# The second 32-column attention: softmax sums and values in bf16 high and low parts instead of fp32

## The chip, the cores and the metric

The kernel runs on one core of a Trainium2 chip. The metric is the device time of one execution in microseconds (us). A core has five engines that run their own instruction streams and meet only at semaphores: TensorE (PE; its weight loads are PEld), VectorE (DVE), ScalarE (ACT), GpSimd (POOL) and SyncE (SP, which starts most DMAs).

## The reference, cut to what matters

The whole kernel is four layers of cross attention and feed forward on x (16 batches of 128 tokens, 128 wide) with a context of 77 keys per batch. The change touches one part, the second attention of the third layer:

```python
# H, D = 16, 32; y is the context: 77 keys of 64 numbers in each of 16 batches
q = jnp.einsum('bsc,hcd->bhsd', xn, wq)
k = jnp.einsum('btc,hcd->bhtd', yn, wk)
v = jnp.einsum('btc,hcd->bhtd', yn, wv)
a = jax.nn.softmax(jnp.einsum('bhsd,bhtd->bhst', q, k) * D ** (-0.5), axis=-1)
o = jnp.einsum('bhst,bhtd->bhsd', a, v)
o = o.transpose(0, 2, 1, 3).reshape(x.shape[0], x.shape[1], H * D)
x_out = x + o @ li1_w + li1_b
```

## The kernel before, in words

The program is a list of stages: L0x, L0m, L1x, L1f, L2a1, L2f1, **L2a2** (this attention), L2f2, L2m, L3x, L3m. All stages write their instructions for each engine by hand; the order in which a function such as `attention` calls its parts is the order on that engine. L2a1 and L2a2 have heads of 32 columns (`A.upright`), L1x has heads of 64.

In a stage of attention a loop runs b from 0 to 19, and each part works on a batch that lags behind it. For L2a2 iteration b holds on TensorE, in this order: `values(b-1)` (v of a batch), `key_scores(b-2)` (L876 and L893, scores in four PSUM banks `ST`), `row_maxima(b, (0, 1))` (L850), `sums(b-3)` (L924: the exponentials times a matrix of ones and zeros, `fourths`, 16 products with fp32 operands), `turn_maxima(b-1)` (L861), up to two projections of a later group of batches, `turned(b-3)` (L940: v times the exponentials, 16 fp32 products), `out_project(b-4)` (L740, 12 products and one of the bias), `row_maxima(b, (2, 3))` (L850), `spread(b-3)` (L952: the reciprocals of the sums, spread over the heads), and one late projection. Projections exist in b = 1 to 3, 5 to 7 and 9 to 11. A product with an fp32 operand leaves two records in the profile, so 16 of them show as x32.

ScalarE makes the exponentials of a batch in two halves (L1598, 77x1024 each), keeps them in fp32 in one of four buffers (`A.PF`), and evacuates PSUM. VectorE does in iteration b: `row_maxima(b, (0, 1))` (L2180 twice), `sums(b-3)` (L2189, the reciprocal, then L2190, the low part of it, with both inputs in SBUF), the low parts of the early projections (L2039), `out_project(b-4)` (L2226, the residual), L2180 twice again for banks 2 and 3, `turned(b-3)` (L2199, outputs times reciprocals). GpSimd does `outputs_lo` (L2857, the low part of the scaled outputs, for which `out_project` on TensorE waits), and now and then `rstd` (L2786 and L2788) for the layer norms. In L1x GpSimd also splits the exponentials: `exponentials_lo` (L2839) takes fp32 exponentials and their upper halves and writes the low halves in bf16.

Apart from the score banks, all results on TensorE go through four PSUM banks in turn. `take` gives a product the next bank and waits until what was in it four takes ago has been read:

```python
def take(*key):
    t = turns.n
    turns.one()
    K.turn[key] = t
    sem.wait_ge(K.emptied[t % 4], t // 4)
    return K.work[t % 4]
```

The takes of an iteration without projections are v, max 0, max 1, sum, negm, o, out, max 2, max 3, scale. So max 2 comes four takes behind sum, whose bank L2190 sets free. With one early projection out is four takes behind sum, with two it is o.

Four records of TensorE that work on different column groups of 32 start together (L924, L940, L952: the four values of i); this text calls them a round.

## Time and profile before

| | |
|---|---|
| median of 3 runs | 1186.53 us (1183.08 to 1191.68) |
| profiled execution | 1188.89 us |
| its span in the profile | 1187.1 us |
| busy in the span: PE / DVE / ACT / POOL | 885.7 / 825.1 / 710.4 / 555.2 us |
| granted TensorE clock, mean of the span | 0.864 |
| batches of L2a2 in full flow | 691 to 796 us of the span |

A row of the timeline is start, length, engine, line, operation, output and inputs by name (`area` is one large SBUF tensor out of which most buffers are cut), shapes, number of instructions merged, and in brackets the idle time before it and what ended it. A merged row's length is from the first start to the last end, and neighbouring rows of a pipelined engine overlap; so what a group costs TensorE is the distance from its start to the start of the next group. A row of --source type gives the minimum, median and maximum length in ns.

### The profile page before, as it was taken

Reading aid. Unit: us, or ns where it says so; the run is one execution under the profiler, and the core shown is the slowest. Engines: PE = TensorE matmul, PEld = TensorE weight load, DVE = VectorE, ACT = ScalarE, POOL = GpSimd, SP = SyncE. Lnnn points to the kernel's source line nnn. Section 1 sums busy time; section 2 is a strip of 40 time slices with the busy share of each in tenths; the row PEclk is TensorE's granted clock in tenths of the full one; section 3 lists DMA queues with packets and bytes.
Section 4 is the critical chain, followed back from the end, with each engine's and each line's share of the span. In section 5 each row is a group of like instructions: output and inputs, shape, how many; then the busy total and the mean of one; then the engine's idle time right before and its main releaser. Section 6 shows DMA issues by size and latency. Waiting matters only on the chain.

```text
span 1187.1 us, 35741 instructions
## 1 busy us (share of the span) xinstructions
PE 885.7 (75%) x14275; PEld 670.4 (56%) x14340; DVE 825.1 (70%) x2234; ACT 710.4 (60%) x1441; POOL 555.2 (47%) x580
## 2 busy tenths in 40 slices
PE   3687658879998664788888488988389865787683
PEld 2465547736777444366666266765278733565573
DVE  4676747888877796678867577757556848666563
ACT  5877546765655665675566566557367684764331
POOL 3474755465567345254452322222551575657334
PEclk9788869988999877799999699989689967876697
DMA  4331142230110101000001000000142221110133
GB/s 110 95 92 31 51 108 80 64 80 28 30 38 20 43 12 49 24 21 12 4 4 46 1 3 4 4 3 2 33 128 73 66 76 41 37 37 24 52 99 88
DMA packets 63040, 53.75 MB, mean 45 GB/s; under 512 B 13915, under 2 KB 51291, under 8 KB 62685
## 3 DMA queue, kind: packets, MB, share of 16 engines
q1 hardware_dynamic: 57100, 42.25, 12.6%
q0 software_dynamic: 4096, 8.40, 2.4%
q8 instruction: 119, 1.95, 0.7%
q10 hardware_dynamic: 1683, 0.81, 0.3%
q14 instruction: 42, 0.34, 0.1%
HBM read 34.22 MB, written 16.25 MB: 43 GB/s over the span
## 4 chain that ended last, share of the span: by engine, by line
PE 36%; DVE 28%; ACT 13%; issue 11%; POOL 7%; DMA 4%; POOLq 1%; ACTq 0%; SPq 0%; DVEq 0%
PE psum L740 12%; PE psum L1324 4%; POOL sorted_in L2990 3%; DVE area L2039 3%; PE psum L1342 2%; DVE stats L2020 2%; PE psum L882 2%; DVE negm L2180 2%; DVE x L2582 1%; DVE area L2212 1%; ACT area L1414 1%; PE psum L964 1%; PE psum L747 1%; ACT xn L1438 1%; DMA area<-sorted_in 1%
## 5 line engine op out<-in xcount | busy, mean ns | idle before, releaser
L1414 ACT ACTIVATE area<-psum 128x512 bf16<-128x512 f32 (+2 forms) x164 | 85.6, 537 | 127.1 <-PE psum L740 66.6
L2039 DVE TENSOR_TENSOR area<-psum,area 128x512 bf16<-128x512 f32 (+3 forms) x156 | 92.7, 618 | 40.0 <-ACT area L1414 38.5
L2793 POOL TENSOR_TENSOR moe<-stage,moe 128x512 bf16<-128x512 f32 x47 | 54.3, 1157 | 110.9 <-ACT moe L1409 110.9
L1598 ACT ACTIVATE area<-psum 77x1024 f32<-77x1024 f32 (+1 forms) x96 | 92.7, 1016 | 22.1 <-PE psum L893 14.4
L2693 DVE TENSOR_TENSOR area<-area 128x512 bf16<-128x512 f32 x106 | 73.9, 702 | 43.8 <-ACT area L1937 31.3
L1324 PE MATMUL psum<-xT_hi,moe 128*128 128x128 bf16 x848 | 98.2, 226 | 5.9 <-issue 3.0
L2786 POOL TENSOR_SCALAR rstd<-moments 128x4 f32<-128x4 f32 (+1 forms) x49 | 13.4, 274 | 153.5 <-DVE moments L2024 150.4
L1324 PE MATMUL psum<-xT_lo,moe 128*128 128x128 bf16 x424 | 84.2, 226 | 0.0
L1342 PE MATMUL psum<-moe,area 128*128 x424 | 83.8, 278 | 0.2
L1324 PEld LDWEIGHTS psum<-xT_hi,moe 128*128 x848 | 76.2, 102 | 10.9 <-issue 7.8
L2920 POOL TENSOR_TENSOR area<-area 128x640 bf16<-128x640 f32 x64 | 79.2, 1259 | 0.5 <-ACT area L1764 0.5
L2180 DVE TENSOR_REDUCE negm<-psum 128x4 bf16<-128x512 f32 (+1 forms) x128 | 68.3, 576 | 13.9 <-PE psum L850 13.5
L1344 PE MATMUL psum<-moe,area 128*128 x424 | 77.4, 222 | 0.0
L2857 POOL TENSOR_TENSOR area<-area 128x512 bf16<-128x512 f32 x32 | 33.3, 1039 | 92.5 <-DVE area L2199 82.6
L2818 POOL DMA_INDIRECT area<-sorted_out,row_index x32 | 35.3, 1103 | 66.7 <-DMA sorted_out<-area 57.9
L1937 ACT ACTIVATE area<-psum,L2be 128x128 f32<-128x128 f32 x184 | 52.5, 368 | 22.4 <-PE psum L1324 22.3
L2839 POOL TENSOR_TENSOR area<-area 77x1024 bf16<-77x1024 f32 x32 | 60.2, 1899 | 6.5 <-ACT area L1598 6.5
L2039 DVE TENSOR_TENSOR xT_lo<-psum,xT_hi 128x512 bf16<-128x512 f32 (+1 forms) x44 | 29.4, 667 | 46.5 <-ACT xT_hi L1414 46.5
L2788 POOL TENSOR_TENSOR rstd<-rstd,cols 128x4 f32<-128x4 f32 (+1 forms) x53 | 59.5, 1123 | 4.4
L2363 DVE TENSOR_REDUCE area<-psum 128x4 bf16<-128x320 f32 x128 | 55.6, 479 | 6.6 <-PE psum L1094 6.6
L740 PE MATMUL psum<-area 128*128 128x128 bf16 (+1 forms) x512 | 45.9, 249 | 18.4 <-DVE area L2474 13.7
L740 PEld LDWEIGHTS psum<-area 128*128 128x128 bf16 (+1 forms) x512 | 42.4, 135 | 23.2 <-issue 22.1
(276 smaller groups left out, 3050.1 us busy)
## 6 DMA issues: line engine op xcount, KB each, us to landing
area<-sorted_in SPq DMA_DIRECT2D x22, 256.0 KB, 3.8
sorted_out<-area SPq DMA_DIRECT2D x22, 256.0 KB, 2.3
stage<-in_w_L0m SPq DMA_DIRECT2D x16, 256.0 KB, 2.8
stage<-in_w_L2m SPq DMA_DIRECT2D x16, 256.0 KB, 2.8
stage<-in_w_L3m SPq DMA_DIRECT2D x16, 256.0 KB, 2.7
sorted_in<-area SPq DMA_DIRECT2D x2, 1472.0 KB, 7.3
stage<-in_w_L2a SPq DMA_DIRECT2D x8, 320.0 KB, 3.4
stage<-in_w_L1x SPq DMA_DIRECT2D x6, 320.0 KB, 3.0
```

What stands on the lines that cost most here:

```text
L740: ins = pe.matmul(out, lhsT, rhs, start=i == 0, stop=i == len(terms) - 1)
L1324: ins = pe.matmul(bank[:, S * c:S * c + S], lhsT, v, start=n == 0, stop=n == 2)
L1342: pe.matmul(both, h_hi, R.w2[c][:, bass.ds(at_w[tile] * 2, 2 * D)], start=R.b2 is None and c == 0, stop=c == FC - 1, skip_group_check=True)
L1344: ins = pe.matmul(high, h_lo, R.w2[c][:, bass.ds(at_w[tile] * 2, D)], start=False, stop=c == FC - 1, skip_group_check=True)
L1414: ins = act.activation(out, bank, ACT.Copy)
L1598: act.activation(A.PF[n % 4][0:A.L, :].rearrange("p (k n) -> p k n", k=2), K.ST[0:A.L, 2 * half:2 * half + 2, :], ACT.Exp, scale=A.scale). ...
L2039: ins = dve.tensor_tensor(out, bank, high, ALU.subtract)
L2180: empty(dve.tensor_reduce(out, bank_of(key)[:, 0:4 * L].rearrange("p (h l) -> p h l", h=4), AX.X, ALU.max, negate=True), key)
L2693: dve.tensor_tensor(R.HL[u], R.HF[u], upper(R.HF[u]), ALU.subtract).then_inc(K.tile_split, tiles.one())
L2788: pool.tensor_tensor(r, r, K.col("half", 0, n)[parts, :], ALU.pow).then_inc(K.rstd_ready, 1)
L2839: pool.tensor_tensor(A.PL[n % 4][0:A.L], A.PF[n % 4][0:A.L, :].rearrange("p (h q) -> p h q", h=8), A.PH[n % 4][0:A.L], ALU.subtract).then_ ...
L2920: pool.tensor_tensor(A.PL[n % 4], A.PF[n % 4], A.PH[n % 4], ALU.subtract).then_inc(K.p_split, 1)
```

## The change

Only L2a2 is changed (`splits=2`; L3x counts its own splits one place later). `A.apart` turns the following on: GpSimd runs `exponentials_lo` for both halves of each batch, as in L1x, between the instructions that it had. VectorE gets `values_lo(b-2)`, which subtracts from the fp32 values their upper halves (77x512, both inputs in SBUF) and sits behind the first pair of row maxima. TensorE's `sums` multiplies `fourths` with the high and the low parts in bf16 (32 products), and its `turned` makes three products for each head: high by high, high by low, low by high (48 products); both wait for `p_split`, and `turned` for `values_apart`.

```diff
+        self.apart = self.upright and splits is not None
+        if self.apart:
+            n = H * hd
+            self.V_hi = [upper(K.carve(V_AT + n * s, n)).rearrange("p (h d) -> p h d", h=H) for s in range(3)]
+            self.V_lo = [K.carve(at, n // 2, BF16).rearrange("p (h d) -> p h d", h=H)
+                         for at in (V_AT + 3 * n, V_AT + 3 * n + n // 2, TMP_AT)]
+            self.fourths_hi = upper(K.carve(OT_AT + n + 384, 128)).rearrange("p (r n) -> p r n", r=4)
...
# TensorE, sums(b)
                 sem.wait_ge(K.exp_done, A.half0 + n + 1)
+                if A.apart:
+                    sem.wait_ge(K.p_split, A.split0 + n + 1)
+                    for k, part in enumerate((A.PH, A.PL)):
+                        for i in range(4):
+                            ins = pe.matmul(bank[32 * i:32 * i + 32, 0:S], A.fourths_hi[0:L, r, :],
+                                            part[n % 4][0:L, 4 * (r % 2) + i, :], start=r == k == 0, stop=r == 3 and k == 1,
+                                            skip_group_check=True)
+                    continue
...
# TensorE, turned(b)
+            if A.apart:
+                sem.wait_ge(K.values_apart, b + 1)
...
+                if A.apart:
+                    sem.wait_ge(K.p_split, A.split0 + n + 1)
+                    v_hi, v_lo, p_hi, p_lo = A.V_hi[b % 3], A.V_lo[b % 3], A.PH[n % 4], A.PL[n % 4]
+                    for k, (v, p) in enumerate(((v_hi, p_hi), (v_hi, p_lo), (v_lo, p_hi))):
+                        for i in range(4):
+                            ins = pe.matmul(bank[32 * i:32 * i + 32, S * c:S * c + S], v[0:L, 4 * c + i, :],
+                                            p[0:L, 4 * (c % 2) + i, :], start=k == 0, stop=k == 2, skip_group_check=True)
+                    continue
...
# VectorE
+        def values_lo(b):
+            for a, _ in A.value_parts():
+                sem.wait_ge(*K.emptied_at((name, "v", b, a)))
+            if b >= 3:
+                sem.wait_ge(K.filled, K.fill[name, "o", b - 3, 0])
+            s = b % 3
+            dve.tensor_tensor(A.V_lo[s][0:A.L], A.Vs[s][0:A.L], A.V_hi[s][0:A.L], ALU.subtract).then_inc(K.values_apart, 1)
...
                 row_maxima(b, (0, 1))
...
+            if A.apart and 0 <= b - 2 < B:
+                values_lo(b - 2)
...
# GpSimd
-        split = mask if A.keys_from_x else exponentials_lo if not A.upright else None
+        split = mask if A.keys_from_x else exponentials_lo if A.apart or not A.upright else None
...
-                       prepare=Normed(K.base, K.res2, wd("ln2g"), wd("ln2b"), 1, also=K.x), affine0=12)
+                       prepare=Normed(K.base, K.res2, wd("ln2g"), wd("ln2b"), 1, also=K.x), affine0=12, splits=2)
-    K.L3x = Dense(K, "L3x", 4, 1, K.x, late=K.L2m, splits=2)
+    K.L3x = Dense(K, "L3x", 4, 1, K.x, late=K.L2m, splits=3)
```

GpSimd's order in the middle of L2a2, before (L2857 is `outputs_lo`, L2802 and L2810 the next group's normed tokens, L2786 and L2788 `rstd`):

```order
L2857 TENSOR_TENSOR area<-area 128x512 x3
L2802 TENSOR_TENSOR area<-area,wide 128x512
L2810 TENSOR_TENSOR x<-x,area 128x512
L2857 TENSOR_TENSOR area<-area 128x512
L2786 TENSOR_SCALAR rstd<-moments 128x4
L2788 TENSOR_TENSOR rstd<-rstd,cols 128x4
L2857 TENSOR_TENSOR area<-area 128x512 x6
```

The same place in the changed kernel, where lines are numbered anew (L2876 is `exponentials_lo`, L2894 `outputs_lo`, L2823 and L2825 `rstd`):

```order
L2894 TENSOR_TENSOR area<-area 128x512
L2876 TENSOR_TENSOR area<-area 77x1024 x2
L2839 TENSOR_TENSOR area<-area,wide 128x512
L2847 TENSOR_TENSOR x<-x,area 128x512
L2894 TENSOR_TENSOR area<-area 128x512
L2876 TENSOR_TENSOR area<-area 77x1024
L2823 TENSOR_SCALAR rstd<-moments 128x4
L2825 TENSOR_TENSOR rstd<-rstd,cols 128x4
L2876 TENSOR_TENSOR area<-area 77x1024
L2894 TENSOR_TENSOR area<-area 128x512
L2876 TENSOR_TENSOR area<-area 77x1024 x2
```

Two splits now stand behind each `outputs_lo`, and where the statistics of the next group come, `rstd` stands between the two splits of a batch.

VectorE's order in one iteration without projections, before:

```order
L2180 TENSOR_REDUCE negm<-psum 128x4 x2
L2189 RECIPROCAL area<-psum 128x128
L2190 TENSOR_TENSOR area<-area 128x128
L2226 TENSOR_TENSOR area<-area,psum 128x128
L2180 TENSOR_REDUCE negm<-psum 128x4 x2
L2199 TENSOR_TENSOR area<-area,psum 128x512
```

And in the changed kernel (L2215 is the row maxima, L2195 `values_lo`, L2224 and L2225 the reciprocal and its low part):

```order
L2215 TENSOR_REDUCE negm<-psum 128x4 x2
L2195 TENSOR_TENSOR area<-area 77x512
L2224 RECIPROCAL area<-psum 128x128
L2225 TENSOR_TENSOR area<-area 128x128
L2261 TENSOR_TENSOR area<-area,psum 128x128
L2215 TENSOR_REDUCE negm<-psum 128x4 x2
L2234 TENSOR_TENSOR area<-area,psum 128x512
```

`values_lo` now stands ahead of the reciprocal; all else is in its old order.

## Rows read from the trace of the kernel before

**Rows 1.** Windows: length, busy us (instructions) by engine, granted clock, DMA share, GB/s.

```profile
691.00:796.00 105.00, 94.35 (x2976) 73.30 (x2978) 75.31 (x182) 67.26 (x118) 25.45 (x29) 0.97 0.02 4
```

**Rows 2.** Timeline of PE, iteration b = 12.

```profile
754.27 0.30 PE L850 MATMUL psum<-area 32*128 32x77 bf16 x8
754.50 1.08 PE L924 MATMUL psum<-area 77*32 77x128 f32 x32
755.40 0.24 PE L861 MATMUL psum<-ident_bf,negm 128*32 128x128 bf16 x4
755.46 1.06 PE L940 MATMUL psum<-area 77*32 77x128 f32 x32
756.45 0.84 PE L740 MATMUL psum<-w_b,area 128*128 128x128 bf16 x12
...
757.29 0.31 PE L850 MATMUL psum<-area 32*128 32x77 bf16 x8
757.53 0.64 PE L952 MATMUL psum<-area,ident_bf 128*32 128x128 bf16 x32
758.09 0.63 PE L740 MATMUL psum<-w_b,ctx2T 128*77 128x512 bf16 x2
...
759.57 0.30 PE L850 MATMUL psum<-area 32*128 32x77 bf16 x8
```

**Rows 3.** Timeline of DVE, the same iteration.

```profile
754.61 0.86 DVE L2180 TENSOR_REDUCE negm<-psum 128x4 bf16<-128x308 f32 x2 [0.65 <-PE psum L850]
755.65 0.96 DVE L2189 RECIPROCAL area<-psum 128x128 f32<-128x128 f32 x1 [0.18 <-PE psum L861]
756.64 0.29 DVE L2190 TENSOR_TENSOR area<-area 128x128 bf16<-128x128 f32 x1
758.41 0.68 DVE L2199 TENSOR_TENSOR area<-area,psum 128x512 f32<-128x512 f32 x1
```

**Rows 4.** Timeline of ACT and POOL, the same iteration.

```profile
754.48 1.93 ACT L1598 ACTIVATE area<-psum 77x1024 f32<-77x1024 f32 x2 [0.43 <-PE psum L893]
...
759.17 1.04 POOL L2857 TENSOR_TENSOR area<-area 128x512 bf16<-128x512 f32 x1 [4.51 <-DVE area L2199]
```

**Rows 5.** Instructions of one line: the split of exponentials in L1x.

```profile
L2839 POOL TENSOR_TENSOR area<-area x32: 1882/1890/1990, 258.1 to 382.3; 77x1024 bf16<-77x1024 f32 x32
```

**Rows 6.** Timeline of DVE: a low part of 512 columns from two SBUF inputs.

```profile
733.60 0.69 DVE L2143 TENSOR_TENSOR xT_lo<-xT,xT_hi 128x512 bf16<-128x512 f32 x1 [1.35 <-ACT xT_hi L1551]
```

**Rows 7.** Instructions of L2190: in L2a1 (480 to 625 us), then in L2a2 (663 to 796 us).

```profile
L2190 DVE TENSOR_TENSOR area<-area x16: 291/814/970, 509.9 to 618.8; 128x128 bf16<-128x128 f32 x16
...
L2190 DVE TENSOR_TENSOR area<-area x16: 291/292/1107, 694.0 to 791.8; 128x128 bf16<-128x128 f32 x16
```

**Rows 8.** Timelines of POOL and DVE where they meet, in L2a1 and then L1x.

```profile
550.62 2.13 POOL L2848 TENSOR_SCALAR_AFFINE_SELECT area<-area 128x1024 f32<-128x1024 f32 x2 [1.07 <-ACT area L1598]
551.94 0.95 DVE L2190 TENSOR_TENSOR area<-area 128x128 bf16<-128x128 f32 x1
...
256.62 1.16 POOL L2793 TENSOR_TENSOR moe<-stage,moe 128x512 bf16<-128x512 f32 x1 [7.67 <-ACT moe L1409]
256.66 1.66 DVE L2576 TENSOR_TENSOR x<-x,moe 128x512 f32<-128x512 f32 x1
258.08 3.84 POOL L2839 TENSOR_TENSOR area<-area 77x1024 bf16<-77x1024 f32 x2 [0.31 <-ACT area L1598]
```

**Rows 9.** Timeline of DVE and PE in b = 10, PE and POOL in b = 7.

```profile
743.45 0.29 DVE L2190 TENSOR_TENSOR area<-area 128x128 bf16<-128x128 f32 x1
...
743.80 1.08 PE L940 MATMUL psum<-area 77*32 77x128 f32 x32 [0.33 <-DVE area L2190]
...
723.14 0.85 PE L740 MATMUL psum<-w_b,area 128*128 128x128 bf16 x12 [0.86 <-DVE area L2190]
...
722.32 1.04 POOL L2788 TENSOR_TENSOR rstd<-rstd,cols 128x4 f32<-128x4 f32 x1
```

**Rows 10.** Timeline of PE in b = 14.

```profile
769.98 1.44 PE L740 MATMUL psum<-w_b,area 128*128 128x128 bf16 x12 [1.25 <-POOL area L2857]
```

More of the change, by code:

```diff
@@ L263, in __init__ @@
         self.var_ready, self.rstd_ready, self.p_split = sem("var_ready"), sem("rstd_ready"), sem("p_split")
+        self.values_apart = sem("values_apart")
         self.p_masked, self.w_split, self.shifted = sem("p_masked"), sem("w_split"), sem("shifted")
@@ L466, in __init__ @@
         self.half0 = 2 * B * number
-        if not self.upright:
+        self.apart = self.upright and splits is not None
+        if splits is not None:
             self.split0 = 2 * B * splits
+        if self.apart:
[3 more added lines that the diff above has]
+                         for at in (V_AT + 3 * n, V_AT + 3 * n + n // 2, TMP_AT)]
+            assert 4 * n <= 2 * V_N
+            self.fourths_hi = upper(K.carve(OT_AT + n + 384, 128)).rearrange("p (r n) -> p r n", r=4)
     def affine_of(self, g, keys):
```

## The prediction

> **What bounds the kernel now.** I looked first at the windows view of the stretch of L2a2 in which batches flow: TensorE is busy for 94.35 of 105 us, VectorE for 75.31, GpSimd for 25.45, at a granted clock of 0.97 [rows 1]. That says that TensorE is full and GpSimd has room, but not which wait decides, so I read the timeline of one iteration without projections, b = 12. TensorE goes through it without a gap: its first maxima start at 754.27 and those of the next iteration at 759.57, a period of 5.30 us [rows 2]. VectorE has waits of its own there, and its L2190 ends at 756.93, 0.36 before TensorE comes to the second maxima at 757.29, for which that end sets the bank free [rows 2, 3]. So TensorE bounds this iteration, and VectorE is 0.36 us from bounding it. In iterations with projections that reserve is gone already: in b = 10 the value products start 0.06 after the end of L2190 and had waited 0.33 for it, and in b = 7 the output product waited 0.86 for it [rows 9].
>
> **What the change takes away.** In fp32 the sums cost 754.50 to 755.40, 0.90 us for 8 rounds, so 0.112 a round; the value products cost 755.46 to 756.45, 0.99 for 8 rounds, so about 0.10 more where column groups give way to full width [rows 2]. L952 is the nearest bf16 form: 8 rounds and the same step to full width in 0.56, so 0.057 a round [rows 2]. The sums become 8 bf16 rounds, 0.46, and save 0.44. The values become 12 rounds, 0.68 and 0.10, and save 0.21. That is 0.65 a batch, 10.4 us over 16 batches: all that there is to win, 0.9% of the time.
>
> **What it adds.** GpSimd gets 32 splits of 77x1024 at 1.89 us [rows 5], 60 us in all; with `outputs_lo` at 1.04 [rows 4] a batch costs it 4.82. That is under the period, so by its own load it is no bound. VectorE gets 16 times `values_lo`. Its form is not in this stage, but L2143, 512 columns from two SBUF inputs, takes 0.69, of which about 0.61 is not overlapped [rows 6]. It stands between the maxima and the reciprocal.
>
> **Where the two meet.** L2190 takes 0.29 us when alone. In L2a1, where GpSimd masks exponentials at the time, its median is 0.81 [rows 7]. One instance shows why: the masks ran 550.62 to 552.75, L2190 was started at 551.94 and ended at 552.89, 0.14 after them [rows 8]. L2576 in L1x, also with two SBUF inputs, was started 0.04 after a GpSimd instruction and ended at 258.32, 0.54 after that one's end at 257.78 [rows 8]. So a VectorE instruction with two SBUF inputs stands still until a reading GpSimd instruction ends. In the other direction, the two L2839 behind it took 3.84 where two of 1.89, overlapping by 0.04, make 3.74: GpSimd, started at 258.08, lost 0.10, so it was let in about 0.14 before VectorE's end [rows 5, 8]. The page "SBUF — State Buffer" of the Trainium skill (section "Who interferes with whom") says that the first to issue holds the shared port pair for the whole instruction; the row has it given back a little earlier. By the page each split would start 0.14 later than I put it, and the sum would be some 2 us higher.
>
> **b = 12 again, changed,** with 754.27 as zero [rows 2, 3, 4]. The maxima end at 1.20 and let the next instruction in at 1.12. `values_lo` runs 1.12 to 1.81. The first half of the exponentials, begun at 0.21, ends at about 1.22 (half of 1.93, with the overlap); GpSimd could start 0.08 later, at 1.30, but gets in at 1.67 and runs to 3.56. The reciprocal runs 1.73 to 2.69. L2190 is started at 2.71, meets the split and ends at 3.56 + 0.14 = 3.70. The second maxima on TensorE start at 3.8, instead of 757.29, which is 3.02. From there to the next first maxima it was 2.28, and still is: 6.08 against 5.30, **0.8 us longer**, though TensorE's own work got 0.65 shorter. Nothing runs over: VectorE's L2199 comes to its end at about 5.6, the second split at 5.6, `outputs_lo` at 6.7, before `values_lo` of the next iteration (7.2) and before the next output product needs it.
>
> **The same for the other iterations.** b = 12, 13 and 15 have this shape: 3 x 0.8 = 2.4. In b = 10 `values_lo` puts the reciprocal 0.34 later, L2190 is started at 743.78 instead of 743.45, the split that began about 742.74 holds it to 744.77, and the value products start at 744.85 instead of 743.80 [rows 9]; they are 0.21 shorter, so the iteration is 0.8 longer. I take that for b = 5, 6, 9, 10, 11: 4.0. In b = 3 and 7 GpSimd's order has `rstd` between the two splits, where L2190 will arrive; its longer part is 1.04 [rows 9], so I take 1.8 each: 3.6. In b = 4 and 14 `rstd` precedes `outputs_lo` on GpSimd and TensorE waits for that already (1.25 us in b = 14 [rows 10]); L2190 meets a split instead of `outputs_lo`: between 0 and 1.89, I take 1.0 each: 2.0. In b = 8 ScalarE holds `spread` back and hides it: 0. In the last three sum iterations there are no maxima, TensorE gains and the two splits of the last batch come in between the exponentials and the sums: +0.4. The sum is **12.4 us** longer. The waits for `values_apart` cost nothing (an iteration of room), nor does `p_split` in full flow: the second split is ready at 5.6, the sums ask for it after 6.3. No DMA moves, and L3x changes a count only.
>
> The profiled execution is 1188.89 (span 1187.1), 2.4 above the median of 1186.53. The sum is against the first, 1201.3; against the median it gives **1199**.
>
> **Rivals.**
>
> *GpSimd wins the race.* `values_lo` is ready at 1.12, the split at 1.30 (b = 12), a margin of 0.18 that goes to zero where another instruction is ahead of the maxima, as L2143 in b = 5 and 9. If the split is first (1.30 to 3.19), `values_lo` ends at 3.19 + 0.54 = 3.73, the reciprocal at 4.61, and L2190 meets the second split (3.6 to 5.5): second maxima at 5.7, period 8.0, 1.9 more than in my forecast. For half of the 13 iterations this is 1211, for all 1224. For it: the margins are small. Against: they are positive in the shape that occurs most. It decides from 0.18 us of delay on VectorE.
>
> *No meeting.* The splits' reads leave room for VectorE, or L2190 falls between them. Then only 0.61 of `values_lo` counts: about 0.1 in the iterations with 0.36 of reserve or with two early projections, 0.6 in b = 3, 7 and 11, +0.4 at the end: some 3 us, 1189.5. Against it: the 0.81 median, and the splits are twice as long as the masks.
>
> *TensorE alone sets the time* (the other side). The bank that L2190 frees must then never be waited for: VectorE would have to lose no more than the 0.36 of reserve that b = 12 has, which it could if ScalarE and TensorE let its later work catch up. Then -10.4: 1176. Against it: the waits of rows 9 exist before anything is added.
>
> *The clock.* After the waits of b = 14 the output products took 1.44 us instead of 0.84, which is the lower level of the clock, 1.2 GHz in place of 2.4 [rows 2, 10]. The new gaps of some 1.3 us per period could bring such stretches; one costs 2 to 4 us. L2a1 has gaps of 0.9 in most iterations; 0 in the sum, and up to 5 in the range.
>
> **How the numbers follow.** Forecast 0.55, with 1192 to 1206 as its own range (unknowns of b = 3, 4, 7, 14 from both ends, the clock). Race lost in many iterations 0.20. No meeting 0.17. TensorE alone 0.08. The range 1183 to 1217 leaves out most of the last and the upper part of the race, together under 0.2. One per cent is about what a measurement of this kernel tells from no change: 1174.7 to 1198.4 counts as the same. Slower: all of the race and 0.30 of the forecast, 0.50. Same: 0.25 of the forecast, 0.17 of no meeting, 0.05 of TensorE alone, 0.47. Faster: 0.03.
>
> **What would show it.** L2225 (was L2190) in L2a2 with a median near 1 us, ending 0.14 after a split; TensorE idle in front of the second maxima, released by it; sums of 0.46 and values of 0.78; a period near 6.1 in b = 12. A `values_lo` of over 2 us says that the race went to GpSimd; one of 0.69 with L2225 at 0.29 says no meeting. I am wrong if the stretch from the sums of b = 12 to those of b = 13 gets shorter.

## The result, and the profile after

The changed kernel took **1204.44 us** (median of 4 runs, 1202.70 to 1206.34), the kernel before beside it 1185.32 (median of 4, 1183.08 to 1191.68). The ratio is 1.0146 with a 95% interval of 1.0113 to 1.0179. The forecast was 1199, 12.4 longer. The medians differ by 19.1 us, and the interval of the ratio, on 1185.32, stands for 13.4 to 21.2. The changed stage itself, from the key scores of b = 2 to those of b = 17, took 102.0 us before and 117.8 after, so **+15.7**. I call it the stage sum, and a period is the distance from the key scores of one b to the next. The two profiled executions differ by 13.8 in span (1187.1 and 1200.9): 15.7 in this stage, less 2.0 in L2a1, whose first periods (b = 2 and 3) are long or short by some 1.9 us from execution to execution in kernels that leave it as it is.

Each stage sum and each period is read from one execution. How far to trust them is shown by the changed kernel and two of the experiments below, which have the same instructions up to b = 11: they took 85.6, 85.4 and 86.5 us from b = 2 to b = 12, while single periods differed by up to 4.7. So differences between stage sums of a microsecond say nothing, and a single long period may be of its execution alone.

Windows view of the changed kernel, batches in full flow; columns as in [rows 1]:

```profile
688.00:810.00 122.00, 94.06 (x3242) 70.65 (x3242) 94.85 (x200) 66.84 (x118) 88.81 (x60) 0.90 0.01 4
```

TensorE is busy as long as before, in a stretch 17 us longer, GpSimd 3.5 times as long, and the granted clock fell from 0.97 to 0.90.

Timeline of TensorE in b = 12 of the changed kernel (L859 are the maxima, L936 the sums, L961 the value products, L749 the output products); it answers to [rows 2]:

```profile
766.69 0.30 PE L859 MATMUL psum<-area 32*128 32x77 bf16 x8
766.92 0.65 PE L936 MATMUL psum<-area 77*32 77x128 bf16 x32
...
767.56 0.36 PE L961 MATMUL psum<-area 77*32 77x128 bf16 x10
768.09 0.75 PE L961 MATMUL psum<-area 77*32 77x128 bf16 x38 [0.17 <-issue]
768.78 0.84 PE L749 MATMUL psum<-w_b,area 128*128 128x128 bf16 x12
...
770.45 0.31 PE L859 MATMUL psum<-area 32*128 32x77 bf16 x8 [0.77 <-DVE area L2225]
...
772.74 0.30 PE L859 MATMUL psum<-area 32*128 32x77 bf16 x8
```

Timeline of VectorE and GpSimd in the same iteration, answering to [rows 3, 4]:

```profile
767.03 0.86 DVE L2215 TENSOR_REDUCE negm<-psum 128x4 bf16<-128x308 f32 x2 [0.65 <-PE psum L859]
767.81 0.68 DVE L2195 TENSOR_TENSOR area<-area 77x512 bf16<-77x512 f32 x1
768.41 0.95 DVE L2224 RECIPROCAL area<-psum 128x128 f32<-128x128 f32 x1
769.39 1.00 DVE L2225 TENSOR_TENSOR area<-area 128x128 bf16<-128x128 f32 x1
...
767.99 4.15 POOL L2876 TENSOR_TENSOR area<-area 77x1024 bf16<-77x1024 f32 x2 [0.91 <-ACT area L1625]
```

Read it from the maxima on VectorE. `values_lo` (L2195) starts at once and takes 0.68. GpSimd's first split is started 0.18 after it and waits for it (2.25 us long instead of 1.89, so it ends at 770.24). The low part of the reciprocals (L2225) is started inside that split and takes 1.00 instead of 0.29. TensorE stands 0.77 us before its second maxima, which begin 3.76 after the first (3.02 before, 3.8 forecast); from there to the next first maxima it is 2.29, as before.

Instructions of the two lines; columns are number, minimum, median and maximum in ns; L2225 is of this stage alone and answers to [rows 7]:

```profile
L2225 DVE TENSOR_TENSOR area<-area x16: 293/998/1686, 692.6 to 805.8; 128x128 bf16<-128x128 f32 x16
...
L2195 DVE TENSOR_TENSOR area<-area x16: 677/678/1949, 682.4 to 798.6; 77x512 bf16<-77x512 f32 x16
```

The median of L2225 went from 0.292 to 0.998, and `values_lo` kept 0.678 in 13 of 16 cases; it took 1.21 and 1.47 in b = 3 and 4, held by other work of GpSimd, and 1.95 at the end. In this execution VectorE won the race in every iteration but the last; one of the experiments below shows that it doesn't always.

The waits view of TensorE, from 688 to 810 us; total us, times, longest:

```profile
PE psum L859 <- DVE area L2225: 7.7, 6, 2.6
PE psum L961 <- DVE area L2225: 6.4, 4, 1.8
PE psum L749 <- DVE area L2225: 3.7, 2, 2.1
```

That is 17.8 us of waits for one instruction, and the same three waits for its predecessor L2190 came to 2.1 us before. Period by period, in us:

| b | before | after | longer | forecast |
|---|---|---|---|---|
| 2 | 6.44 | 6.03 | -0.4 | 0 |
| 3 | 7.18 | 9.63 | 2.5 | 1.8 |
| 4 | 7.12 | 8.23 | 1.1 | 1.0 |
| 5 | 7.70 | 8.81 | 1.1 | 0.8 |
| 6 | 7.64 | 11.05 | **3.4** | 0.8 |
| 7 | 6.99 | 8.17 | 1.2 | 1.8 |
| 8 | 6.86 | 6.87 | 0.0 | 0 |
| 9 | 7.70 | 8.81 | 1.1 | 0.8 |
| 10 | 7.10 | 10.40 | **3.3** | 0.8 |
| 11 | 6.10 | 7.65 | 1.6 | 0.8 |
| 12 | 5.30 | 6.05 | 0.8 | 0.8 |
| 13 | 5.77 | 6.05 | 0.3 | 0.8 |
| 14 | 9.39 | 9.08 | -0.3 | 1.0 |
| 15 | 6.37 | 6.05 | -0.3 | 0.8 |
| 16 | 4.37 | 4.88 | 0.5 | 0.4 |

Two iterations stand out. TensorE in b = 10, then VectorE in b = 6:

```profile
752.39 1.47 PE L961 MATMUL psum<-area 77*32 77x128 bf16 x48 [1.79 <-DVE area L2225]
753.79 1.46 PE L749 MATMUL psum<-w_b,area 128*128 128x128 bf16 x12
...
716.45 1.69 DVE L2225 TENSOR_TENSOR area<-area 128x128 bf16<-128x128 f32 x1
```

After a wait of 1.79 us the value products took 1.47 instead of 0.88 and the output products 1.46 instead of 0.84: the lower level of the clock, 1.2 GHz (granted 0.55 from 752 to 756 us, 1.00 in the four before). In b = 6 the split had begun 0.35 before L2225 and not 1.0, so it held L2225 for 1.69, and the same drop followed.

### The profile page after: what moved, and what is told of

Read it like the earlier page. It is cut to its first block, busy times and chain, and to the rows that moved or that the text cites. A ratio compares the mean times of both kernels' runs of the same rounds, so it can differ in the third digit from the quotient of the medians.

```text
span 1200.9 us, 36394 instructions
## 1 busy us (share of the span) xinstructions
PE 889.7 (74%) x14596; PEld 665.8 (55%) x14596; DVE 845.2 (70%) x2250; ACT 709.9 (59%) x1441; POOL 621.4 (52%) x612
## 4 chain that ended last, share of the span: by engine, by line
PE 34%; DVE 29%; ACT 13%; issue 10%; POOL 8%; DMA 4%; POOLq 1%; ACTq 0%; SPq 0%; DVEq 0%
PE psum L749 13%; PE psum L1351 3%; POOL sorted_in L3027 3%; DVE area L2066 3%; DVE stats L2047 2%; DVE negm L2215 2%; PE psum L1369 2%; DVE area L2225 2%; DVE area L2224 2%; ACT xn L1465 2%; PE psum L979 1%; PE psum L891 1%; DVE x L2619 1%; DVE area L2247 1%; ACT area L1441 1%
## 5 line engine op out<-in xcount | busy, mean ns | idle before, releaser
L1441 ACT ACTIVATE area<-psum 128x512 bf16<-128x512 f32 (+2 forms) x164 | 85.6, 537 | 133.0 <-PE psum L749 72.9
L2876 POOL TENSOR_TENSOR area<-area 77x1024 bf16<-77x1024 f32 x64 | 125.5, 1977 | 28.7 <-ACT area L1625 28.6
L2823 POOL TENSOR_SCALAR rstd<-moments 128x4 f32<-128x4 f32 (+1 forms) x49 | 13.4, 273 | 143.1 <-DVE moments L2051 140.0
L2215 DVE TENSOR_REDUCE negm<-psum 128x4 bf16<-128x512 f32 (+1 forms) x128 | 68.3, 577 | 13.6 <-PE psum L859 13.0
L2825 POOL TENSOR_TENSOR rstd<-rstd,cols 128x4 f32<-128x4 f32 (+1 forms) x53 | 59.5, 1123 | 4.4
L749 PE MATMUL psum<-area 128*128 128x128 bf16 (+1 forms) x512 | 47.1, 252 | 18.8 <-DVE area L2511 14.1
L3027 POOL DMA_INDIRECT sorted_in<-w_b,row_index x32 | 36.2, 1131 | 41.1 <-DVE row_index L2692 32.8
L2894 POOL TENSOR_TENSOR area<-area 128x512 bf16<-128x512 f32 x32 | 33.6, 1051 | 44.4 <-DVE area L2234 34.4
```

The lines of the kernel that those rows point to most:

```text
L749: ins = pe.matmul(out, lhsT, rhs, start=i == 0, stop=i == len(terms) - 1)
L1441: ins = act.activation(out, bank, ACT.Copy)
L2215: empty(dve.tensor_reduce(out, bank_of(key)[:, 0:4 * L].rearrange("p (h l) -> p h l", h=4), AX.X, ALU.max, negate=True), key)
L2876: pool.tensor_tensor(A.PL[n % 4][0:A.L], A.PF[n % 4][0:A.L, :].rearrange("p (h q) -> p h q", h=8), A.PH[n % 4][0:A.L], ALU.subtract).then_ ...
L3027: pool.indirect_dma_start(R.rows_in[half], bass.IndirectOffsetOnAxis(ap=K.row_index[:, c, HB * half + b:HB * half + b + 1], axis=0), R.nor ...
```

## The experiments

Theory A is that of the prediction: `values_lo` moves the reciprocal back and a split then holds its low part, so that the bank comes free late. Theory B: the split on GpSimd is not what costs the time; it is lost on VectorE by `values_lo` alone or on TensorE, by more and shorter products. Theory C: the clock, lowered by the new waits, costs most of what A leaves unexplained.

| kernel | median us | ratio to before, 95% | stage sum us |
|---|---|---|---|
| before | 1185.32 | 1 | 102.0 |
| after | 1204.44 | 1.0146 (1.0113 to 1.0179) | 117.8 |
| products alone | 1189.26 | 1.0030 (1.0005 to 1.0054) | 103.1 |
| no splits | 1196.34 | 1.0074 (1.0048 to 1.0100) | 109.1 |
| no values_lo | 1197.16 | 1.0095 (1.0066 to 1.0125) | 112.7 |
| low part from PSUM | 1199.59 | 1.0109 (1.0048 to 1.0169) | 113.2 |
| sums twice | 1208.20 | 1.0164 (1.0130 to 1.0199) | 120.4 |
| clears ahead of values_lo | 1204.21 | 1.0125 (1.0080 to 1.0170) | 118.7 |
| chained clears | 1269.45 * | 1.0215 (1.0158 to 1.0273) | 128.0 |
| before, bank freed early | 1187.02 | 0.9989 (0.9967 to 1.0010) | 100.3 |
| after, early and late | 1199.01 | 1.0093 (1.0066 to 1.0120) | 114.6 |
| before, low part from PSUM | 1242.71 * | 1.0014 (0.9983 to 1.0044) | 103.5 |
| after, from PSUM and late | 1252.60 * | 1.0092 (1.0059 to 1.0125) | 109.8 |

Each ratio is to the kernel before as it ran beside: 1185.76 us for the four from "products alone" to "low part from PSUM", 1188.69 for the next two and for the two with "early", so rows of different groups compare by ratio. The three with a star ran together, and there the kernel before took 1241.42 us; the stage sum of the one built on it is 103.5, so the rest lies outside this stage. "Clears ahead" has two runs.

**Products alone: neither splits nor values_lo.** TensorE makes all its products from high parts; the low parts' share of the result is left out.

```diff
-                    for k, part in enumerate((A.PH, A.PL)):
+                    for k, part in enumerate((A.PH, A.PH)):
...
-                    for k, (v, p) in enumerate(((v_hi, p_hi), (v_hi, p_lo), (v_lo, p_hi))):
+                    for k, (v, p) in enumerate(((v_hi, p_hi), (v_hi, p_hi), (v_hi, p_hi))):
...
-            if A.apart and 0 <= b - 2 < B:
-                values_lo(b - 2)
...
-        split = mask if A.keys_from_x else exponentials_lo if A.apart or not A.upright else None
+        split = mask if A.keys_from_x else exponentials_lo if not A.upright else None
```

> From the changed kernel, both additions are left out: no splits, no values_lo; TensorE makes the same 80 bf16 products a batch from high parts only (the low parts' share is left out). This prices what TensorE's shorter work is worth by itself: 0.65 us a batch where TensorE sets the period, less where L2225 still frees the bank late. Both theories: 1176 to 1179 us, and b = 12 at 4.7.

1189.26 us, where 1176 to 1179 was expected: TensorE's shorter work is worth nothing by itself. Timeline of TensorE in b = 3 and b = 12 (L957 the value products), then its waits from 680 to 800 us:

```profile
694.21 1.47 PE L957 MATMUL psum<-area 77*32 77x128 bf16 x48
...
757.62 0.47 PE L957 MATMUL psum<-area 77*32 77x128 bf16 x18
758.62 0.64 PE L957 MATMUL psum<-area 77*32 77x128 bf16 x30 [0.54 <-issue]
...
PE psum L957 <- issue: 3.3, 3, 1.8
PE psum L975 <- ACT area L1637: 2.5, 2, 1.5
```

TensorE stopped 0.54 us in the middle of the value products, waiting for nothing that the profile shows ("issue"), and the period was 5.57, not the 4.7 expected. From b = 3 on such stalls came to 3.6 us in the stage (0.8 before), and ScalarE's evacuations held it 2.5 us where 1.0 was before (two of the three stalls of L957 in the last lines, 1.8 and 0.9, come from b = 17 on). And TensorE ran at 1.2 GHz through b = 3 (1.47 for the value products) into b = 4: those two periods were 1.8 us longer than before. Expectation and prediction both had TensorE's instructions follow each other as closely when there are more of them. They didn't. That the products by themselves cost the 19 us is refuted (0.3%, at most 0.5), but their gain is gone too.

**No splits on GpSimd**

```diff
-                    for k, part in enumerate((A.PH, A.PL)):
+                    for k, part in enumerate((A.PH, A.PH)):
...
-                    for k, (v, p) in enumerate(((v_hi, p_hi), (v_hi, p_lo), (v_lo, p_hi))):
+                    for k, (v, p) in enumerate(((v_hi, p_hi), (v_hi, p_hi), (v_lo, p_hi))):
...
-        split = mask if A.keys_from_x else exponentials_lo if A.apart or not A.upright else None
+        split = mask if A.keys_from_x else exponentials_lo if not A.upright else None
```

> From the changed kernel, GpSimd's 32 splits of the exponentials are left out; TensorE makes as many bf16 products as before, but uses the high parts of the exponentials where the low parts stood (the low parts' share of the result is left out). values_lo on VectorE stays. Theory A (a split holds L2225 until it ends): nothing holds L2225 now, its median in L2a2 is 0.29, b = 12 gets a period of about 5.4, only values_lo is paid for: 1188 us, near the kernel before. Rival B (the load of values_lo ahead of the reciprocal is what costs): values_lo is still there, so most of the 19 us stays: 1200. Rival C (the half clock rate of b = 6 and 10 has its own cause): those two iterations stay at 10 us and more.

Between the two values: 1196.34. In b = 12 VectorE's low part (L2223) is back at 0.29, and the period at 5.52. But around b = 3 and 4 TensorE shows this:

```profile
766.99 0.29 DVE L2223 TENSOR_TENSOR area<-area 128x128 bf16<-128x128 f32 x1
...
697.44 0.44 PE L859 MATMUL psum<-area 32*128 32x77 bf16 x8 [2.06 <-DVE area L2223]
...
703.33 1.50 PE L959 MATMUL psum<-area 77*32 77x128 bf16 x48
```

With no GpSimd in its way in b = 3 (0.68 for `values_lo`), `values_lo` and the statistics still put the low part so late that TensorE waits 2.06 us, and then works at 1.2 GHz into b = 4 (period 9.22, before 7.12). So `values_lo` without splits costs 6.0 us of stage over the products alone, 4.6 of them in b = 3, 4 and 7 (8.85, 9.22 and 9.59, with the products alone 8.35, 7.71 and 6.99). In b = 4 and 7 GpSimd is in its way even so, though not with a split: `values_lo` took 1.44 and 1.22 there, each ending 0.54 to 0.55 after an `outputs_lo` of GpSimd. The prediction had priced no such meeting:

```profile
703.29 1.44 DVE L2193 TENSOR_TENSOR area<-area 77x512 bf16<-77x512 f32 x1
703.15 1.04 POOL L2892 TENSOR_TENSOR area<-area 128x512 bf16<-128x512 f32 x1
```

The part of B on `values_lo` holds beside A: neither has all of it.

**Splits, but no values_lo.** The low part of the values is left out of the result.

```diff
-            if A.apart and 0 <= b - 2 < B:
-                values_lo(b - 2)
...
-                    for k, (v, p) in enumerate(((v_hi, p_hi), (v_hi, p_lo), (v_lo, p_hi))):
+                    for k, (v, p) in enumerate(((v_hi, p_hi), (v_hi, p_lo), (v_hi, p_hi))):
```

> From the changed kernel, values_lo on VectorE is left out and the third product uses the high part of the values (the low part's share of the result is left out). The splits on GpSimd stay. Theory A: the reciprocal comes 0.6 earlier, but L2225 is now requested early in the first split and stands until that split's end: in b = 12 the split runs 1.30 to 3.19, the second maxima start at 3.4, period 5.7; in all 0.4 us a batch less than the changed kernel, 1198 us. Rival B (load of values_lo): 1185 or less.

1197.16 us, and 5.69 for b = 12. VectorE and TensorE there:

```profile
765.42 1.24 DVE L2223 TENSOR_TENSOR area<-area 128x128 bf16<-128x128 f32 x1
...
766.72 0.31 PE L859 MATMUL psum<-area 32*128 32x77 bf16 x8 [0.54 <-DVE area L2223]
```

The low part starts earlier in the split and stands longer (1.24), but ends sooner. The splits cost 9.6 us of stage over the products alone, `values_lo` 6.0, both 14.7: the two add, nearly. The medians say the same with less chance in them: 0.65% and 0.44% over the products alone, together 1.09, and 1.16 for the changed kernel.

**Low part of the reciprocals from PSUM**

```diff
-            chained(dve.reciprocal(A.RF[b % 2], bank_of(key)[:, 0:S]))
-            empty(dve.tensor_tensor(low, A.RF[b % 2], high, ALU.subtract), key)
+            bank = bank_of(key)[:, 0:S]
+            chained(dve.reciprocal(bank, bank))
+            chained(dve.tensor_copy(high, bank))
+            empty(dve.tensor_tensor(low, bank, high, ALU.subtract), key)
```

> From the changed kernel, splits and values_lo kept, results complete. The reciprocal is written back to its PSUM bank, VectorE copies the high part from there to SBUF in bf16 (about 0.27) and takes the low part from PSUM and SBUF (0.29), so that it has one SBUF input; this is so in L2a1 as well. Theory A: the low part is never held any more; in b = 12 the second maxima start at about 3.3 instead of 3.8, period 5.55; no long idle stretches in b = 6 and 10; and L2a1, where L2225 took 0.81 in the median, gains some 0.2 a batch: 1192 us. Rival B (load on VectorE): 0.27 more for each of 32 batches, 1207 to 1212 us.

1199.59, where 1192 was expected; b = 12 took 5.68 (expected 5.55). VectorE, then TensorE:

```profile
771.09 0.30 DVE L2226 CAST area<-psum 128x128 bf16<-128x128 f32 x1
771.42 0.29 DVE L2227 TENSOR_TENSOR area<-psum,area 128x128 bf16<-128x128 f32 x1
...
771.77 0.31 PE L859 MATMUL psum<-area 32*128 32x77 bf16 x8 [0.81 <-DVE area L2227]
```

With one of its inputs in PSUM the low part takes 0.29 in the middle of a split (769.69 to 773.78): the hold is a matter of two SBUF inputs, as the prediction had it. But taking it away gives back only 4.6 of the 15.7 us. The chain is still late by `values_lo` and by the copy.

**Sums made twice**

```diff
-            for r in range(4):
+            for r in list(range(4)) * (2 if A.apart else 1):
```

> The changed kernel, but TensorE makes the 32 products of sums twice in L2a2 (same result), 0.46 us a batch. In b = 12 the sums are needed only when values_lo is through (1.73), and twice they are ready at 1.35, so nobody waits for them. Theory A (L2225 held by a split, TensorE only waits): the work falls into TensorE's waits, b = 12 stays at 6.05, and the total within 3 us of 1204.4. Theory C (part of the loss is the clock at its lower level, 24.6 us of it in L2a2 against 14.2 before, because TensorE waits so long in b = 6 and 10): fuller TensorE keeps the upper level, b = 6 and 10 fall from 11.05 and 10.4 to about 8.7 and 8.1, total 1199. Rival B (TensorE's instruction stream is the bound): 7 us more, 1212.

TensorE in b = 6 and, further on, in b = 13:

```profile
721.48 0.88 PE L961 MATMUL psum<-area 77*32 77x128 bf16 x48 [1.76 <-DVE area L2225]
...
774.93 0.75 PE L936 MATMUL psum<-area 77*32 77x128 bf16 x39 [0.93 <-issue]
```

In b = 6 the wait is the same 1.76 us, with 0.46 us more work ahead of it, and the clock stayed at 2.4 GHz: the period is 9.00, 2.05 shorter than after, and 8.5 without the added sums. So 2 of the 3.4 us of b = 6 are the clock, which confirms C for the price at this place. That the added work kept the clock up is not shown: in b = 13 of the same run TensorE fell to 1.2 GHz behind a wait of 1.53 us with the same added work ahead of it, and the next experiment shows the wait of 1.76 without added work and without a fall. In total nothing was won: the added work, new stalls and the low clock in b = 13 took it back.

**Four clears ahead of values_lo** in b = 12, 13 and 15

```diff
             if A.apart and 0 <= b - 2 < B:
+                for i in range(4 if b in (12, 13, 15) else 0):
+                    dve.memset(K.recip[:, b % 2, 4 * i:4 * i + 4], 0.0)
                 values_lo(b - 2)
```

> The changed kernel, with four small VectorE memsets (about 0.07 us each) ahead of values_lo in b = 12, 13 and 15 alone, which use up the margin of 0.18 us by which values_lo comes before the first split. The prediction's rival said: the split then runs first (1.30 to 3.19), values_lo ends at 3.7 and takes some 2.4 us, L2225 meets the second split, and the period goes from 6.05 to 8.0. If who comes first does not matter, the period grows by the 0.3 us of the memsets. Total 1204 + 5.7 = 1210 by the first, 1205 by the second.

VectorE in b = 12:

```profile
767.30 0.07 DVE L2299 MEMSET recip<- 128x4 f32 x2
767.32 0.68 DVE L2195 TENSOR_TENSOR area<-area 77x512 bf16<-77x512 f32 x1
```

The clears overlapped with `values_lo` and delayed it by some 0.05 us, not 0.25 (1.17 from TensorE's first maxima, 1.12 in the changed kernel). So the edit tested nothing. But in this execution the race was lost in b = 5, where nothing is edited. VectorE, GpSimd and TensorE in b = 5, then TensorE in b = 6 and 10:

```profile
705.93 2.06 DVE L2195 TENSOR_TENSOR area<-area 77x512 bf16<-77x512 f32 x1
705.55 4.19 POOL L2878 TENSOR_TENSOR area<-area 77x1024 bf16<-77x1024 f32 x2 [0.94 <-ACT area L1625]
709.94 1.46 PE L961 MATMUL psum<-area 77*32 77x128 bf16 x48 [2.79 <-DVE area L2225]
...
721.37 0.87 PE L961 MATMUL psum<-area 77*32 77x128 bf16 x48 [1.76 <-DVE area L2225]
...
754.83 0.89 PE L961 MATMUL psum<-area 77*32 77x128 bf16 x48 [1.79 <-DVE area L2225]
```

The split began 0.38 us before `values_lo`, which took 2.06; TensorE waited 2.79 us for the low part, fell to 1.2 GHz, and the period was 13.46 instead of 8.81. It is a place that the rival had named, where another instruction of VectorE stands ahead of the maxima (L2170 here, L2143 before); in the changed kernel `values_lo` won there by 0.05 us. And b = 6 and 10, unedited too, had the very waits of the changed kernel, 1.76 and 1.79, with no fall behind them: 8.57 and 7.94 instead of 11.05 and 10.40. From the start of the value products to the end of the period that is 2.05 us in b = 6 (the other 0.4 lies ahead of them, where the low part was held for 1.09 instead of 1.69) and 2.5 in b = 10: the price of the fall. Which wait a fall follows changes from one execution to another, and why is not shown.

**Six clears, each waiting for the one before**

```diff
             if A.apart and 0 <= b - 2 < B:
+                for _ in range(6 if b in (12, 13, 15) else 0):
+                    chained(dve.memset(K.recip[:, b % 2, 0:4], 0.0))
                 values_lo(b - 2)
```

> The changed kernel with six clears of 4 columns, each waiting for the one before, ahead of values_lo in b = 12, 13 and 15, so that values_lo comes after GpSimd has begun its first split. The rival 'GpSimd wins the race' says what then happens: values_lo is held to the end of the first split and ends 0.54 after it (its length from the start 2.0 to 2.5 us), the reciprocal follows, its low part meets the second split, and the period is 8.0 us in b = 12 instead of 6.05, so some 6 us for the three iterations over the changed kernel (1.020 of the kernel before). If the race has no such price (VectorE is let in between the reads of the split), values_lo keeps 0.68 and the period grows by the clears alone, 0.3 to 0.5 us each: some 1 us in all.

GpSimd, VectorE and TensorE in b = 12, where TensorE's first maxima began at 785.13:

```profile
786.44 4.19 POOL L2878 TENSOR_TENSOR area<-area 77x1024 bf16<-77x1024 f32 x2 [0.92 <-ACT area L1625]
...
787.04 1.84 DVE L2195 TENSOR_TENSOR area<-area 77x512 bf16<-77x512 f32 x1
788.80 0.94 DVE L2224 RECIPROCAL area<-psum 128x128 f32<-128x128 f32 x1
789.78 1.00 DVE L2225 TENSOR_TENSOR area<-area 128x128 bf16<-128x128 f32 x1
...
790.83 0.31 PE L859 MATMUL psum<-area 32*128 32x77 bf16 x8 [3.12 <-DVE area L2225]
```

Now GpSimd is first. `values_lo` lasts from 787.04 to 788.88, 0.55 past the end of the first split (786.44 and 1.89), and the second maxima stand 5.70 after the first, as the rival had worked out. The periods of b = 12, 13 and 15 are 8.66, 8.89 and 8.91: the rival's 8.0, and more where the clock fell behind the wait of 3.12. So the price of a lost race is real: 2.6 to 2.9 us an iteration over the changed kernel, the clears (0.72) and the clock in it. In b = 12 the margin of 0.18 us is what keeps the changed kernel from paying it; in b = 5 the run with four clears paid it unforced.

**The kernel before, with the bank freed by the reciprocal.** The bank is set free after the reciprocal, and the spread waits for the low part by a semaphore of its own.

```diff
-            chained(dve.reciprocal(A.RF[b % 2], bank_of(key)[:, 0:S]))
-            empty(dve.tensor_tensor(low, A.RF[b % 2], high, ALU.subtract), key)
+            empty(dve.reciprocal(A.RF[b % 2], bank_of(key)[:, 0:S]), key)
+            sem.wait_ge(*K.emptied_at(key))
+            dve.tensor_tensor(low, A.RF[b % 2], high, ALU.subtract).then_inc(K.recips_split, 1)
```

> The kernel before (fp32 products), with one edit: the bank of the sums is set free by the reciprocal (L2189) and no longer by L2190 behind it; spread, which needs the low part, waits for a semaphore of its own. In L2a1 L2190 stands behind GpSimd's masks (median 0.81) and TensorE waits for it 12 times in the two stages. Theory A (what hurts is that a held instruction guards a bank): TensorE's waits for L2190 in front of L850, L940 and L740 go away in L2a1 and L2a2 both, some 5 us: 1180. If the reciprocal itself or another wait comes right behind: no change, 1185.

The ratio is 0.9989, no change that the measurement can tell (its interval reaches from 3.9 us shorter to 1.2 longer). The two stages it touches were shorter: L2a2 by 1.8 us, L2a1 113.4 instead of 117.4. Of the latter 2.0 are the first two periods, which vary in kernels that leave L2a1 as it is (115.4 to 117.5 in all); the rest comes with the edit: b = 12 took 5.96 instead of 6.18, b = 5 took 8.72 instead of 9.28. The profiled execution, 1182.98, was one of the shortest of twelve, so the stages may flatter it.

**The changed kernel, with that and values_lo behind the outputs**

```diff
+            if A.apart and 0 <= b - 2 < B:
+                values_lo(b - 2)
             if not A.upright and b >= 4:
                 turn_outputs(b - 4)
```

(and the three lines of the experiment before)

> The changed kernel, results complete, with two edits: the bank of the sums is set free by the reciprocal, as in before_early, and values_lo moves on VectorE to behind the scaled outputs (L2234), where VectorE waited. Theory A: L2225 is still held by the first split (to about 3.3 in b = 12), but only spread waits for it: b = 12 at 5.4, the iterations with projections 0.8 less than in the changed kernel, no long idle stretches: 1188 to 1192. If the holding itself, wherever it stands, costs the time (VectorE's queue behind it): 1200.

1199.01 us, stage 114.6. VectorE and TensorE in b = 12, then TensorE's waits over the stage (L2067 is the low part of a projection):

```profile
767.21 1.05 DVE L2227 TENSOR_TENSOR area<-area 128x128 bf16<-128x128 f32 x1
...
766.77 0.23 PE L871 MATMUL psum<-ident_bf,negm 128*32 128x128 bf16 x2 [0.72 <-issue]
...
PE psum L860 <- DVE area L2067: 5.2, 6, 1.9
```

L2227 is still held for 1.05 us, but hardly anyone waits for it. The time went to the next in line: to L2067, now behind `values_lo`, and to issue stalls, 5.5 us. The longest period is b = 8, 10.83 instead of 6.87: at its new place `values_lo` met a split and an `outputs_lo` behind it and took 2.37 us, TensorE waited 1.91 for L2067, and the low clock followed. One wait was traded for others.

**The kernel before, low part from PSUM** (the edit shown above, on the kernel before)

> The kernel before, with the reciprocal left in its bank and its low part made with one input from PSUM, in L2a1 and L2a2. The chain of three gets one short copy longer (0.2 us) and no VectorE instruction in it has two SBUF inputs. If GpSimd's hold on the low part is what costs time in L2a1 (median 0.81 instead of 0.29 us there), L2a1 gets up to 0.5 us a batch shorter where that is waited for, less 0.2 for the copy: its 117.4 us become 113 to 115, L2a2 keeps its 102, the total is 2 to 4 us below the kernel before (0.997 to 0.998). If TensorE's own stream fills what the waits leave, as the products alone did, no change: 1.000.

Instructions of the low part (L2192), both stages:

```profile
L2192 DVE TENSOR_TENSOR area<-psum,area x32: 291/292/293, 524.2 to 807.6; 128x128 bf16<-128x128 f32 x32
```

All 32 take 0.29, in L2a1 too, where the masks held the median to 0.81 [rows 7]. The ratio is 1.0014, no change, and L2a1 took 117.5, as before. Yet its single periods moved, the copy included: those of b = 6, 9 to 13 and 15 fell by 0.3 each (6.18 to 5.87 in b = 12), 2.1 us together, so there the hold had cost more than the copy does. b = 14 took 1.5 back. TensorE there, in this kernel and then in the kernel before:

```profile
612.26 1.10 PE L740 MATMUL psum<-w_a,area 128*128 128x128 bf16 x12 [1.05 <-POOL area L2859]
...
599.49 0.83 PE L740 MATMUL psum<-w_a,area 128*128 128x128 bf16 x12 [1.05 <-POOL area L2857]
```

The granted clock was 0.58 from 612 to 616 us, where it had stayed at 1.00 before; with the low part from PSUM in the changed kernel, the same b = 14 kept its 8.26 and L2a1 took 114.1.

**The changed kernel, low part from PSUM and values_lo late** (both edits above, without the bank freed early)

> The changed kernel with both: the low part of the reciprocal has one PSUM input, and values_lo stands last in VectorE's iteration, so that nothing in the chain of maxima, reciprocal and low part has two SBUF inputs and that chain is 0.2 us longer than before by the copy alone. If all that the change costs comes through that chain, the stage from b = 2 to 17 falls from 117.8 us to about 103 to 105 (that of the kernel with the products alone, 103.1, and the copy), 1.003 to 1.005 of the kernel before. If values_lo, now longer where it meets a split, holds the next maxima instead, the stage stays at 109 to 114 and TensorE's waits are for L2215.

The stage took 109.8 us, the least of all versions that keep the change's arithmetic, and still 7.8 over before; the ratio, 1.0092, is no better than that of the version with early and late (1.0093). TensorE waited 4.0 us for the maxima behind `values_lo`, as the expectation's second case had it, but still 5.8 for the low part of the reciprocals (L2227), at three places. The largest entry of its waits, and a stall in b = 13:

```profile
PE psum L749 <- DVE negm L2215: 2.4, 3, 1.0
...
780.06 0.62 PE L749 MATMUL psum<-w_b,area 128*128 128x128 bf16 x8 [1.02 <-issue]
```

No version beat the kernel before by more than the measurement can tell.

## Why the prediction was right, and where it was not

- **The chain that decides, right.** In b = 12 every step that decides came within 0.1 us: `values_lo` 0.68 (forecast 0.69), the split behind it, L2225 inside the split, second maxima at 3.76 (3.8), period 6.05 (6.08). That two SBUF inputs are the reason is shown by the low part with a PSUM input, 0.29 beside a split. That both halves of the chain matter is shown by leaving out either one: 6.0 and 9.6 us of stage, 14.7 together.
- **When the split lets go.** L2225 was started at 769.39 and ended at 770.39. The first split ended at 770.24, 0.15 before that; the forecast had 0.14. Taking its own 1.89 off, it was let in at 768.35, 0.14 before the end of `values_lo` (768.49), as forecast too. The page "SBUF — State Buffer" of the Trainium skill ("Who interferes with whom") has the pair held for the whole instruction; the traces agree within 0.15 us for these two and disagree for another (next point).
- **`rstd` between the splits, wrong.** The sum had 1.0 us extra each for b = 3 and 7. GpSimd's `rstd` (L2825) and VectorE's low part met in b = 7 as forecast; GpSimd's row and VectorE's:

```profile
729.20 1.04 POOL L2825 TENSOR_TENSOR rstd<-rstd,cols 128x4 f32<-128x4 f32 x1
...
729.24 0.30 DVE L2225 TENSOR_TENSOR area<-area 128x128 bf16<-128x128 f32 x1
```

  L2225 was not held at all. An instruction of GpSimd that reads 4 columns doesn't hold VectorE for its 1.04 us. b = 7 became 1.2 longer instead of 1.8. b = 3 became 2.5 longer, by a wait of 2.57 us for L2225, which came late behind `values_lo` (1.21 long, held by L2847 of GpSimd) and the statistics, and by the low clock behind it.
- **The clock, mis-sized.** It stood in the sum with 0 and in the range with up to 5 us. It took 2.05 us in b = 6 (by the sums made twice and by the run with four clears alike) and 2.5 in b = 10 (by the latter, which had the same waits there without the fall). b = 3 ends with such rows too. In exchange the low stretch behind b = 14, which before reached into b = 15 (6.37), ended earlier; that is why b = 14 and 15 got 0.3 shorter each, where 1.8 more was forecast for the two.
- **b = 6 and 10: the term "0.8 each for b = 5, 6, 9, 10, 11".** It measured 1.1, 3.4, 1.1, 3.3 and 1.6, 10.5 us instead of 4.0: the largest error of the sum. 4.5 of the missing 6.5 are the clock. What is not the clock in it is L2225 arriving at another point of the split: 1.69 long in b = 6. In the run with four clears, with the upper level in both, b = 6 and 10 were 0.9 and 0.8 longer than before, as forecast, so for these two the step was right and the term lacked the price of the clock.
- **TensorE's own gain, wrong in meaning.** The prediction used -0.65 a batch inside the iterations and 10.4 us as all that there was to win. The sizes were right (sums 0.48 and values 0.81 where no stall fell into them), but products alone gave 0 of the 10.4. In b = 12 a stall of 0.54 us, and in b = 3 and 4 the low clock, took what the shorter products had saved. The rival "TensorE alone sets the time" fell with it: even without splits and without `values_lo`, its 1176 was missed by 13 us.
- **The sum.** 12.4 forecast, 15.7 in the stage, 13.8 between the profiled spans, 19.1 between the medians. Overestimates for b = 7, 13, 14 and 15 and underestimates for b = 3, 5, 6, 9, 10 and 11 partly cancel. The forecast of 1199 landed 5.4 us below the measured 1204.44, by its mechanism and its b = 12, not by all its terms; 12.4 itself lies just under the measured interval of 13.4 to 21.2, and that it came no further off is in part luck.
- **The rivals.** "No meeting" is refuted by the median of 0.998. "GpSimd wins the race" happened fully in one batch only of the changed kernel's profiled execution, at the end (1.95). In another execution with the same instructions up to there it happened in b = 5 and cost 4.7 us, the clock in it; forced in three, it cost what was worked out, the clears and the clock. So this rival is no alternative to the forecast but a part of it that comes and goes. How often it comes is not known: of the three profiled executions with the same instructions up to b = 11, one had it there.

**What stays open.** The issue stalls of TensorE (3.6 us with the products alone, 5.5 in the version with both moves). They are rare in the kernel before (one of 0.52, in b = 17), whose sums and values leave 64 records of products a batch, and come to 3.6 us in the stage with the products alone, which leave 80; whether the number of instructions, their shortness or something else is the cause was not tried apart. Open too is why the clock fell behind a wait of 1.76 us in one execution and not in another, and which part of the 5.4 us between forecast and median lies in races lost.

## What to carry to other kernels

Before you move work to an engine that is idle, list the instructions of its neighbour that read two operands from SBUF, and follow each one's last reader: a short one that frees a bank (0.29 us here) is worth more protection than a long one. A saving on the busiest engine is worth something only if no wait lies within it: check the distance to the next wait in each kind of iteration, not the busy share (0.36 us of reserve here against 0.65 of saving). And when the forecast makes new waits on TensorE like the ones of 1.76 and 1.79 us here, put a price on the clock behind them (2 to 2.5 us each where it fell), not only into the range. A margin of 0.05 or 0.18 us between two engines is no margin: give the lost race a share in the sum.

## What the runs showed of the hardware

- VectorE's subtraction of 128x128 fp32 took 0.29 us alone, 0.29 with one input in PSUM beside a split, and with two inputs in SBUF beside one up to 1.69 (2.02 with the sums made twice). The first split, when it had to wait for VectorE, showed up to 2.38 instead of 1.89.
- GpSimd's operation on 128x4, 1.04 us long, did not hold the same VectorE instruction (0.30), in b = 3 and in b = 7.
- After waits of 1.76 and 1.79 us TensorE's next 60 products ran at 1.2 GHz in the changed kernel (1.43 and 1.46 us instead of 0.88 and 0.84, in b = 6). After the same two waits in another execution of the same instructions they ran at 2.4 (0.87 and 0.84). The fall cost 2.05 and 2.5 us.
- VectorE's subtraction of 77x512 fp32, both inputs in SBUF, took 0.68 us alone; started behind a GpSimd instruction of 128x512 or 77x1024, it ended 0.54 to 0.55 us after that one's end (1.44, 1.84).
- TensorE stopped for 0.5 to 1.8 us in the middle of a group of short products with nothing in the profile to wait for.
- Clears of 4 columns took 0.07 us each and overlapped with the next instruction; chained by waits, six of them took 0.72.
